# Third layer's mixture of experts: eight dense experts against two gathered by row number

## The reference

```python
# x: (B, S, D), B = 4, S = 748, D = 128; E = 8 experts, hidden width 512, K = 2
# pooled = softmax over the sequence of (x @ attn_w + attn_b), times x, summed over S
# g (B, E): softmax of the gate's logits of pooled, kept for the 2 largest, renormalised, zero for the other 6
h  = gelu(einsum('ebsd,edh->ebsh', x, w1) + b1[:, None, None, :], approximate=False)
eo = gelu(einsum('ebsh,eho->ebso', h, w2) + b2[:, None, None, :], approximate=False)
return einsum('ebso,be->bso', eo, g)
```

## Time and profile before

| | us |
|---|---|
| median of 3 runs (lowest, highest) | 4555.29 (4553.76, 4556.07) |
| span of the profiled execution | 4551.8 |
| PE busy in the span | 4137.7 |
| ACT busy | 2872.1 |
| DVE busy | 2766.0 |
| POOL busy | 708.1 |

### The profile page before, as it was taken

One profiled execution on the slowest core, in us unless ns is written; L12 is line 12 of the kernel. 1 busy time (PEld: TensorE's weight loads), 2 busy tenths in 40 slices (PEclk: granted clock), 3 DMA queues, 4 the chain that ended last, 5 costly groups with the idle time before them and its releaser, 6 DMA issues.

```text
span 4551.8 us, 67714 instructions
## 1 busy us (share of the span) xinstructions
PE 4137.7 (91%) x25107; PEld 2324.2 (51%) x25107; DVE 2766.0 (61%) x6426; ACT 2872.1 (63%) x6118; POOL 708.1 (16%) x484
## 2 busy tenths in 40 slices
PE   7787599999999999999999999868889888988988
PEld 5464344444444444444444444435556555655666
DVE  5656477777777777777777777422442444344254
ACT  3232278777877787777878787674664574474533
POOL 1000212232322222222222232100000000000000
PEclk9878699999999999999999999989999999999999
DMA  2000233333424242424243333000000000000000
GB/s 109 7 21 1 43 45 47 46 52 45 60 43 61 37 60 43 60 39 54 43 53 56 48 50 41 24 32 28 32 1 24 22 1 15 27 1 1 29 4 4
DMA packets 94713, 160.46 MB, mean 35 GB/s; under 512 B 18305, under 2 KB 75058, under 8 KB 94130
## 3 DMA queue, kind: packets, MB, share of 16 engines
q1 hardware_dynamic: 94386, 156.14, 20.6%
HBM read 73.97 MB, written 7.82 MB: 18 GB/s over the span
## 4 chain that ended last, share of the span: by engine, by line
PE 74%; DVE 9%; issue 6%; ACT 6%; DVEq 2%; PEld 1%; POOL 1%; PEldq 0%; DMA 0%; POOLq 0%; SPq 0%; ACTq 0%
PE ps L1190 12%; PE ps L1226 12%; PE ps L1200 10%; PE ps L1556 9%; PE ps L1260 4%; PE ps L1269 4%; PE ps L1181 2%; PE ps L1077 2%; PE ps L1688 2%; PE ps L1488 2%; PE ps L1289 2%; PE ps L1626 1%; DVE peaks L2274 1%; PE ps L1650 1%; PE ps L1062 1%
## 5 line engine op out<-in xcount | busy, mean ns | idle before, releaser
L2274 DVE TENSOR_REDUCE peaks<-ps 128x1 f32<-128x748 f32 (+1 forms) x1536 | 1408.8, 933 | 482.4 <-PE ps L1200 459.5
L1845 ACT ACTIVATE masked<-ps 128x384 f32<-128x384 f32 (+3 forms) x1536 | 683.7, 486 | 193.6 <-PE ps L1190 181.1
L1845 ACT ACTIVATE probs<-ps 128x384 f32<-128x384 f32 (+1 forms) x1536 | 662.4, 484 | 73.9 <-PE ps L1190 73.7
L923 POOL TENSOR_TENSOR rstd<-var,minus_half 128x6 f32<-128x6 f32 x104 | 138.4, 1331 | 2823.8 <-DVE var L2500 1495.0
L1190 PE MATMUL ps<-shared 98*128 98x384 bf16 (+3 forms) x1536 | 447.6, 327 | 4.5 <-ACT probs L1845 1.7
L1190 PE MATMUL ps<-q_stack,k_stack 98*128 98x384 bf16 (+3 forms) x1536 | 450.3, 328 | 1.2
L1200 PE MATMUL ps<-k_stack,q_stack 96*128 96x374 bf16 (+1 forms) x1536 | 380.6, 329 | 35.3 <-DMA k_stack<-parts 21.8
L1200 PE MATMUL ps<-shared 96*128 96x374 bf16 (+1 forms) x1536 | 372.1, 323 | 7.4 <-DVE peaks L2274 6.9
L1190 PEld LDWEIGHTS ps<-shared 98*128 98x128 bf16 (+1 forms) x1536 | 148.0, 103 | 337.2 <-ACT masked L1845 126.2
L1190 PEld LDWEIGHTS ps<-q_stack,k_stack 98*128 98x128 bf16 (+1 forms) x1536 | 149.6, 103 | 329.9 <-ACT masked L1845 121.2
L1200 PEld LDWEIGHTS ps<-k_stack,q_stack 96*128 96x128 bf16 (+1 forms) x1536 | 154.8, 105 | 157.6 <-DVE peaks L2274 42.2
(11 more groups left out here) (584 smaller groups left out, 7646.7 us busy)
## 6 DMA issues: line engine op xcount, KB each, us to landing
shared<-parts SPq DMA_DIRECT2D x192, 187.0 KB, 9.1
wr<-in_l SPq DMA_DIRECT2D x32, 580.5 KB, 3.5
q_stack<-parts SPq DMA_DIRECT2D x96, 187.0 KB, 8.0
k_stack<-parts SPq DMA_DIRECT2D x96, 187.0 KB, 10.5
wts<-in_l SPq DMA_DIRECT2D x32, 514.5 KB, 3.6
wrow<-in_l_rows SPq DMA_DIRECT2D x32, 320.0 KB, 4.0
wq<-in_l SPq DMA_DIRECT2D x32, 192.0 KB, 3.4
shared<-in_tv SPq DMA_DIRECT2D x1, 4096.0 KB, 27.1
```

What stands on the lines that cost most here:

```text
L923: pool.tensor_tensor(lane.rstd, lane.var, minus_half[:, :], ALU.pow).then_inc(S["rstd_ready"], 1)
L1845: act.activation(probs_ring(u)[0:m, 0:hi - lo], src[0:m, 0:hi - lo], ACT.Exp, scale=float(HD) ** -0.5).then_inc(S["ring_done"], 1)
L2274: v.tensor_reduce(peaks[0:m, g, j, head:head + 1], src[0:m, :, 0:T // 2], XY, ALU.max)\
```

## The change

Part 1 now has two experts in place of eight. For each sequence DVE turns the two chosen ranks into row numbers, POOL fetches the rows with an indirect DMA, and the merge uses two gate values of their own.

```diff
+TOP = 2
@@ tail_steps, part 1
-        steps = []
-        for e in range(E):
+        steps = [(("fuse", LATE), 12.0)] if b == 0 else [(("picked",), 5.0)]
+        for e in range(TOP):
             steps += [(("up2", e, i), 1.35) for i in range(FT)] + [(("down2", e, i), 2.6) for i in range(2)]
         steps.append((("back2",), 3.0))
-        return steps + norm_steps("h", *([(("fuse", LATE), 12.0)] if b == 0 else []))
+        return steps + norm_steps("h")
@@ sync: load_second and its calls (8 for each sequence) are gone
-                sp.wait_ge(S["wts_free"], n.take("wts_free"))
-                sp.dma_start(wts[:, e % 2, 0:W2_END], A["l2"][e, :, :]).then_inc(S[f"wts_loaded{e % 2}"], 16)
@@ gpsimd
+            pool.iota(past_rows[:, :], [[1, 1]], base=E * P, channel_multiplier=1, allow_small_or_imprecise_dtypes=True)
...
+            def load_second(lane, k):
+
+                pool.wait_ge(S[f"picked_{k}"], n.take(f"picked_{k}"))
+                for i in range(TOP):
+                    pool.wait_ge(S["wts_free"], n.take("wts_free"))
+                    pool.indirect_dma_start(wts[:, i, 0:W2_END], None, second_rows,
+                                            bass.IndirectOffsetOnAxis(ap=lane.picks[:, i:i + 1], axis=0))\
+                        .then_inc(S[f"wts_loaded{i}"], 16)
+
             for b, part, (what, *at) in TAIL:
                 if what == "normalise":
                     power(1, tails[b % 2])
+                elif part == 0 and what == "gate" and at[0] == 1:
+                    load_second(tails[b % 2], b % 2)
@@ vector, gating_parts (for the third layer's gate only)
                 first_of_largest(L, PK)
+                if picks is not None:
+                    step(v.tensor_scalar(picks[:, 0:1], M, -float(P), past_rows[:, 0:1], ALU.mult, ALU.add))
                 yield
...
                 step(v.tensor_reduce(M, CD, X, ALU.max))
+                if picks is not None:
+                    step(v.tensor_scalar(picks[:, 1:2], M, -float(P), past_rows[:, 0:1], ALU.mult, ALU.add))
+                    v.drain().then_inc(S["picked" + of], 1)
...
+                if picks is not None:
+
+                    own = gates[:, :, 0:tiles].rearrange("p e t -> p t e")
+                    step(v.tensor_tensor(PK, PK, CD, ALU.subtract))
+                    for i, one in enumerate((PK, CD)):
+                        step(v.tensor_tensor(L2, own, one, ALU.mult))
+                        step(v.tensor_reduce(pick_gates[:, i:i + 1], L2, X, ALU.add))
@@ vector, merge2: the gate comes from lane.pick_gates[:, e:e + 1]; the column copy is gone
-                    column(lane, e, 1)
```

More of the change, by code:

```diff
@@ L113 @@
     "spread0", "spread1", "taken0", "taken1", "heads_ready", "heads_done", "slot_ready", "slot_done",
-    "logits_ready", "exps_ready", "operand_ready")]
+    "logits_ready", "exps_ready", "operand_ready", "picked")]
 class Tally:
@@ L518 @@
     gcol: object
+    picks: object
+    pick_gates: object
 def cut(ap, n):
@@ L596, in audio_tower @@
         gcol = sb("gcol", [P, NT])
+        picks = sb("picks", [P, LANES, TOP], mybir.dt.int32)
+        past_rows = sb("past_rows", [P, 1])
+        pick_gates = sb("pick_gates", [P, LANES, TOP])
         q_room = q_stack0[:, :, :].rearrange("p e t -> p (e t)").bitcast(F32)
@@ L704, in lane_small @@
             return dict(stats=stats_s[:, k, :, :], mv=mv_s[:, k, :, :], var=var_s[:, k, :], rstd=rstd_s[:, k, :],
-                        half_sum=half_sums[:, k, :], pooled=pooled_s[:, k, :], **small(k))
+                        half_sum=half_sums[:, k, :], pooled=pooled_s[:, k, :], picks=picks[:, k, :],
+                        pick_gates=pick_gates[:, k, :], **small(k))
         tails = (
@@ L907, in _ @@
                     load_hn(b + 1)
-                for e in range(E):
-                    load_second(e)
                 store(b - 1)
@@ L1566, in second @@
                         base[k] = n.now(f"feat_done_{k}")
-                        n.take(f"feat_done_{k}", 2 * (FT + 1) * E)
+                        n.take(f"feat_done_{k}", 2 * (FT + 1) * TOP)
                     if what == "up2":
@@ L2603, in gate @@
                     if i == 0:
-                        gating[k] = gating_parts(1 if part == 0 else NT, part == 0, *lane.gating, lane.gates, f"_{k}")
+                        chosen = (lane.picks, lane.pick_gates) if part == 0 else ()
+                        gating[k] = gating_parts(1 if part == 0 else NT, part == 0, *lane.gating, lane.gates, f"_{k}",
+                                                 *chosen)
                     next(gating[k])
                 def merge2(lane, k, e):
-                    column(lane, e, 1)
                     v.wait_ge(S[f"feat_done_{k}"], n.take(f"feat_done_{k}", 2 * (FT + 1)))
+                    gate = lane.pick_gates[:, e:e + 1]
                     if e == 0:
-                        v.tensor_scalar(sum2[:, 0:T], outs2[0][:, 0:T], lane.gcol[:, 0:1], None, ALU.mult)
+                        v.tensor_scalar(sum2[:, 0:T], outs2[0][:, 0:T], gate, None, ALU.mult)
                     else:
-                        v.scalar_tensor_tensor(sum2[:, 0:T], outs2[e % 2][:, 0:T], lane.gcol[:, 0:1], sum2[:, 0:T],
+                        v.scalar_tensor_tensor(sum2[:, 0:T], outs2[e % 2][:, 0:T], gate, sum2[:, 0:T],
                                                ALU.mult, ALU.add)
@@ L2618, in back2 @@
                 def back2(lane, k):
-                    merge2(lane, k, E - 1)
+                    merge2(lane, k, TOP - 1)
                     ready(k)
```

6 lines of the change are left out of this document (2 added, 4 removed).

## The result

The changed kernel takes 4327.09 us (median of 4 runs, 4322.85 to 4334.77) against 4554.97 (4 runs, 4553.76 to 4556.07), a ratio of 0.9500 [0.9487, 0.9514]: 5% faster. The forecast was 4333 in a range of 4310 to 4357. The profiled execution took 4329.91 us, its span 4328.1.

A forecast was written before the change was run, and what follows sets the result against it. PE's issue was taken as the bound. Gains of 48.7 us at sequence 0 and 57.8 in each of three woven stages (173.4) made 222 us, so 4555.3 - 222 = 4333 us, range 4310 to 4357.

The forecast's parts named there:

- What is removed: Six of eight experts for each of four sequences: 241.2 us of PE, 60.3 in each of four stages.
- Sequence 0: Part 1 of sequence 0: first expert waits for gate and gather, about 11 us later; the stage gains 48.7 us.
- The moved fuse: At sequence 0, inside the 11 us before the first expert: it gives nothing at its old place.
- The norm's wait, uncovered: Begin of each woven stage: fourth layer's transposes wait for DVE and POOL without experts as filler; loss 5.8 us.
- The gate's end: Each woven stage, at PE's last weighing: seven more small DVE steps, 1.7 us lost.
- The end, gained: End of each woven stage: waits of `back2` (2.21 us) and the last norm's transposes (3.55); gain 5.8 us.
- The clock: Each woven stage: less low clock after its end, 1.5 us gained, between 0 and 4 possible; its begin unchanged.
- Waits within: Each woven stage: table loads for the fourth gate's exponentials and the `up4` and `down4` biases show on PE; 2.3 us lost.
- The sum: Whole kernel: 48.7 us at sequence 0 and 173.4 in three woven stages, 222 us off 4555.3, so 4333 us.
- POOL's queue: Gathers hold POOL, delaying the power for the fourth layer's norm; at 10 us a gather about 4376 us; chance 0.10.
- PE starved: Woven stages: fourth-layer jobs each lose 0.57 us to an activation, 18 us a stage, so 4388 us; chance 0.06.
- Slower: Gathers hold POOL at sequence 0 and in woven stages; at 32.6 us a gather the 222 us are gone; chance 0.02.

The follow-up runs named there:

- four passes: Changed kernel with each gathered expert computed twice for each sequence, the two gathers kept: 4407.97 us.
- the fuse back: Changed kernel with the fuse of heads 4 to 7 at its old place, the norm behind sequence 0's experts: 4335.29 us.
- the filled order: Changed kernel with the first expert's four `up2` steps ahead of the fourth layer's norm in each woven stage: 4314.60 us, again 4314.86.
- 16 in line: Changed kernel with 14 more gathers of 64 bytes a row on POOL's queue in each sequence, behind the two real ones: 4370.38 us.
- the early merge: The filled order with DVE's merge of the second expert moved ahead of a fourth-layer `down4` step: 4311.01 us.
- the gate cut in two: Gate's last 13 DVE steps moved behind PE's last weighing: 4334.53 us on the changed kernel, 4317.97 us on the filled order.
- the first pair of kernels: The changed kernel, 4327.09 us, and the same with the fuse back, 4335.29 us.
- the second (4.3 us): The filled order, 4314.86 us beside it, and the same with the fuse at its old place, 4319.14 us.

## Why the prediction was right, point by point

- **What is removed.** 24 experts of 10.05 us: right. The records are gone, and half an expert still takes 5.03, in the changed kernel and with four passes.
- **Sequence 0.** Predicted 48.7 us of gain, measured 49.9. POOL's gather began 5.6 us behind the gate's matmul, against 5.35 to the signal in the sum; from its begin to the first expert took 4.7 us, against 6.5. The instruction took 1.23 us (1.4 assumed), and the first gather landed in 4.5 us. The 1.5 us of sharing with the 2060 KB load fell on the second gather instead: it left at 3110.87, 0.07 us ahead of that load, and landed in 8.4 us, but in 5.1 us with the fuse back, where the load leaves at 3145.30. Its expert begins only at 3126.80, so this is hidden. PE waited 5.3 us and not 3.6 in two other kernels' profiled executions, so landing varies by about as much. The first half expert ran at the low clock (7.75 us to the next row against 5.03), but that of before did too (a row of 7.57 in the earlier trace rows), so little of this is new; the transposes behind the longer idle time took 1.54 us for 0.88, as assumed.
- **The moved fuse.** "It gives nothing at its old place" is right in the stretch that the sentence speaks of (44.24 against 43.56). As a statement on the whole time it was wrong: undoing it costs 7.6 us, and 4.3 in the filled order, where the runs overlap. The step looked only at the waits near the move; the difference is in granted clock later.
- **The norm's wait, uncovered.** Predicted 5.8, measured 5.75.
- **The gate's end.** Predicted 1.7, measured 5.69 less the 4.11 of the earlier trace rows, 1.6. The seven steps fall ahead of the weighing, so they show in the stretch before the stage. They belong to the price of choosing at run time, once for each woven stage.
- **The end, gained.** Predicted 5.8, of which 3.55 came. **This is the step that failed:** "several steps of part 3 stand between these and what they wait for" holds for PE's order and the last norm. For `back2` it is DVE's order that decides: its merge stands behind a `down4` whose operands PE has just made. The wait is 2.17 us where it was 2.21. Moving the merge alone removed it.
- **The clock.** Predicted 1.5 us of gain a stage, between 0 and 4. Behind the first stage the first chain of the next takes 8.81 us (3474.60 to 3483.41) where it took 12.83: 4.0 gained. Behind the other two it had taken 11.44 and 11.45, and the gain is 2.6. At the stage's begin the prediction has the low clock "before and after alike", which was wrong: with the idle time of 5.75 us behind another of 5.69, the clock is at 0.50 from 3382 to 3399 and from 3403 to 3406, some 20 us, where it had been so for about 7 (3431 to 3438). The three stretches behind the stages are 2.7 to 3.0 us shorter; in the first two the next gate's end is already taken off.
- **Waits within.** Predicted 2.3 us. The first woven stage is 56.4 shorter; 60.3 less 5.75 and plus 3.55 would be 58.1, so 1.7 is left for these waits and the clock at the begin together. In the other two stages the same sum leaves 2.0 and -0.6, so 3.1 us in all where 6.9 were allowed. The waits themselves can be read in the first stage: the expert matmuls (L1568) wait 2.2 us for ACT, where those of before (L1556) waited 1.2, and 1.05 us for DVE at L1719 is new. That is 2.05 us more, close to the 2.3.
- **The sum.** For the woven stages 171.2 in them, 8.4 behind them and 2.1 lost ahead of the first, so 177.5, with 173.4 predicted. The failed 2.25 us a stage, 6.75 in all, were made good elsewhere. What was left for the waits within and the clock at the begin was 3.1 us in place of 6.9. Between the stages 6.3 us were gained, where the gate's end and the end's clock together should have lost 0.6. So part of the closeness is luck. The 1.0 us lost in the last part and the 2.7 ahead of the gate had no term. Two signs were off: the second woven stage took 89.76 us where 84 to 88 was said, and a wait was left at the stages' ends. The terms named for the high end of the range add up to 4355, and not to its 4357.
- **Rivals.** POOL's queue: in a woven stage a gather holds it for 1.33 us at most, with the gap (3383.76 to 3385.09), where it had to exceed 4.35 to matter. The largest bound, one from the power's 0.22 us for a value, was far off, since a gather's rows are not handled at that rate. PE starved: in the three woven stages the expert matmuls waited for ACT for 2.2, 1.7 and 2.2 us, where the rival had 18 a stage, and half an expert of the third layer kept its 5.03 us, also with four passes. Slower: never near.

The Trainium skill's "GPSIMD Engine Reference" ("Performance pitfalls for Q7 kernels") led to an estimate of 10.9 us a gather, for small reads of 102 cycles for each index. The trace does not agree: 0.94 to 1.23 us for 128 indices, also with 16 in line. The section speaks of what a kernel on GpSimd's own processors pays, and here it did not describe an indirect DMA. The Trainium skill's "DMA: Bandwidth & Descriptors" ("Anatomy of one DMA — SWDGE (gpsimd) path") gave an estimate of 3.2 us. The measured 4.2 to 8.4 us, median 4.8, is above it in all eight.

## What to carry to other kernels

Where a gate picks a few experts for a whole tile of work, compute only those. Row numbers made on DVE and an indirect DMA cost about 1 us of GpSimd's queue and 5 us to landing, and only the first use, which has nothing to hide behind, paid for them (5.6 us of 4328). The small DVE steps for row numbers and gate values cost 1.6 us more where PE waited for that gate, ahead of the first woven stage. Once filler is gone, read every wait again in the order of the engine that is waited for, not only of the one that waits: `back2`'s wait and the gate's end were settled on DVE. Then fill the waits that the removal has uncovered: the filled order took 13 us less than the changed kernel, and the version with the early merge had the lowest median of all, 4311 us, though its runs overlap those of the filled order.

## What the runs showed of the hardware

- An indirect DMA's price on GpSimd did not depend on its bytes: 0.94 to 1.13 us for 128 rows of 64 bytes and 0.94 to 1.23 for 128 rows of 4116 bytes, 0.30 us apart. No run had another number of rows. It landed in 4.2 to 8.4 us with 514.5 KB, the 8.4 beside the 2060 KB load, and the kernel before had 3.6 at the median for the same bytes from SP.
- In the changed kernel and its variants (those with the gate cut in two left out) the same 1352 or 1353 matmul records of an attention stretch took 233.8 to 235.9 us at a mean granted clock of 0.95 or 0.96, 236.4 to 237.5 at 0.94, and 238.7 to 239.8 at 0.93. Which of these came changed between executions of one kernel: in the filled order the same stretch took 236.48 us in one and 239.6 in the other. A woven stage moved likewise within one execution, that with the fuse back: 90.3 at 0.87 for the first and 86.9 at 0.91 for the third. So a difference under 5 us says little unless the stage itself shows it.
- With the fuse back, and with the gate cut in two, the granted clock was 0.50 for 15.7 and 15.9 us behind the norm's wait in the first woven stage, with PE at work without a gap. In the changed kernel it was 0.50 for 4.1 us there, full for some 3.7, 0.50 once more for 3.3, and then full.
- Why the fuse's place makes the low clock more frequent later stays open. In the first pair of kernels (7.6 us) it was seen in stretches with unchanged instructions. In the second (4.3 us) the runs overlap and the profiled execution does not show the loss. The link between the fuse and the clock was not tested.
